# LoRA B of the first phase read by fours of experts over all 128 partitions, with small orders changed on four engines

## The chip, the cores and the metric

The kernel runs on one core of a Trainium2 chip. The metric is the device time of one execution in microseconds (us), as the median of three runs. A core has a matrix engine (TensorE, PE in the profile), three engines for elementwise work (VectorE or DVE, ScalarE or ACT, GpSimd or POOL), and a SyncE (SP) that here only issues transfers. All engines run their own program in order and meet through semaphores. Sixteen DMA engines move data between HBM, the on-chip buffer SBUF (128 partitions) and back.

## The reference, cut to what matters

Two layers act on x of 32 x 64 x 1024 floats. The first, which holds the change, is

```
y   = agg_w(cond) @ x + agg_b(cond)                 # a mixing matrix and a bias per batch entry
A_eff = einsum('bn,nri->bri', gate, lora_A)         # 16 experts, rank 32, 8 groups b
B_eff = einsum('bn,nor->bor', gate, lora_B)         # lora_B: 16 experts x 1024 outputs x 32 ranks
x   = x + y @ kernel + bias + B_eff (A_eff y) + lora_B_shared (lora_A_shared y)
```

The second layer is a grouped convolution of x with a bias from cond, a gated product (w12, silu) and an output product (w3), added to x. All is computed to float32 accuracy: each operand of a large product is split into a high and a low part, and three products of parts are added.

## The kernel before, in words

There are four stages: the first layer (to about 250 us), the convolution, the gated product and the output product. The change lies in the first 60 us, where the operands of the first layer are made.

**Weights.** The 1024 x 1024 kernel is loaded in eight blocks of 128 rows (`load_wk(k)`, 512 KB each) into four slots `raw`. ACT copies a block into its high part (`wk_hi_part`, L808), DVE subtracts to get the low part (`wk_lo_part`, L1062; POOL does block 0, L726) and then frees the slot. Slot 0 is used by block 0, then by the shared LoRA B (`RAW_LBS`), then by block 7; blocks 4, 5 and 6 take slots 1, 2 and 3 after blocks 1, 2 and 3.

**LoRA A.** `la_result(0..3)` on PE multiplies the gates with LoRA A; `la_hi_part` (ACT, L791) and `la_lo_part` (DVE, L1057) split the results.

**LoRA B.** Its output index is split into z, b and e (2 x 32 x 16 values). It is read in two halves z of 1 MB each, into `lb_raw[z]` of 128 partitions x 8 KB. Partition 32a + b holds, for the four experts 4a + n, the 16 outputs e of block b. Before, one DMA per a fills 32 partitions with four runs of 2 KB each. DVE turns each half with 8 transposes in two calls (`turn_lora_b`, L1153), calls 2 and 3 for half z = 1 and calls 0 and 1 for half z = 0. `lb_result_mm(0..3)` on PE multiplies with the gates: 0 and 1 need turns 2 and 3, and 2 and 3 need turns 0 and 1 as well. `lb_hi_part` (ACT, L820) and `lb_lo_part` (DVE, L1158) split the four results.

**Shared LoRA B.** 32 partitions x 4 KB; DVE turns it (L1173), ACT and POOL make its high and low part.

**PE.** After two tiles of y (`y_tile(0)`, `y_tile(1)`: y of 128 rows each, in banks 0 and 1), the first two row tiles go through their eight k steps `first_u(a, k)` one block of weights at a time, between the LoRA products. `first_u(0, 0)` writes bank 2 and so waits for `bias_made` 2, the convolution's bias `cb_c`, which DVE takes from that bank. `first_u(1, 0)` writes banks 4 and 5, and waits until DVE has made `la_lo_part(0)` and `(1)` from them. After k = 7 come `z_group(0)` and the steady loops.

**SP's order.** SP issues nearly every transfer of this phase, in one order, and waits in it for slots. After `wk_lo_part(6)` frees a slot (wait before `load_x(3, 3)`, L382) come the rest of y's bias (L430), the first group's LoRA B rows (`first_group_lb`, L358), b3, the eight stores of LoRA B to `lora_b_scratch` (L438), x tiles 4 and 5, then a wait for these stores and the loads of the next group's LoRA B (L455, L457), for which PE waits in `u_tile(2, ...)`. ACT issues the second half of the first group's rows.

Of the kernel before, what the change touches and what calls it, by code (L numbers as in the profile page):

```python
# [26 lines left out]
ALU = mybir.AluOpType  # L27
# [4 lines left out]
NB, NC, NL = 32, 64, 1024  # L32
# [7 lines left out]
NLORA, RANK = 16, 32  # L40
# [3 lines left out]
PH, BLK = 8, NL // 8  # L44
# [6 lines left out]
def layered_kernel(nc, x, cond, fside, c0_w0, c0_b0, c0_w1, c0_b1, c0_w2, c0_b2, c0_weight, c0_bias_k,  # L51
# [17 lines left out]
    with ctx:  # L69
        BASE = -(-nc.sbuf_base // 64) * 64  # L70

        def at(name, shape, kb, dt=F32):

            return nc.alloc_sbuf_tensor_at(name, shape, dt, offset=BASE + int(kb * 1024))

        def sem(name):
            return ctx.enter_context(nc.semaphore(name))
# [55 lines left out]
        def tiny(name, shape):  # L133
            k = next(small)
            for _ in range(-(-4 * int(np.prod(shape[1:])) // 32) - 1):
                next(small)
            return at(name, shape, k / 32)
# [4 lines left out]
        fside_s = tiny("fside_s", [NB, NC])  # L142
        yb_c, cb_c = tiny("yb_c", [NB, NC]), tiny("cb_c", [NB, NC])
# [60 lines left out]
        def bank(n, k=1):  # L204
            return ps[:, n * HALF:(n + k) * HALF]
# [24 lines left out]
        bias_mm, bias_made = sem("bias_mm"), sem("bias_made")  # L230
# [15 lines left out]
        lb_in = [sem(f"lb_in{c}") for c in range(2)]  # L246
# [45 lines left out]
        RAW_LBS, QUART = 4, HALF // 2  # L292
# [7 lines left out]
        def wait_slot(eng, n):  # L300

            if n in POOL_WK:
                eng.wait_ge(wk_lo_pool, n + 1)
            else:
                eng.wait_ge(raw_free, n + 1 - len(POOL_WK))


        lb_raw = [at(f"lb_raw{s}", [P, 2 * NL], k) for s, k in enumerate((144.25, 82))]
# [55 lines left out]
        def _(sp):  # L364
            def load_raw(n, src, rows=P):
                if n >= 4:
                    wait_slot(sp, n - 4)
                sp.dma_start(raw[n % 4][0:rows, :], src).then_inc(raw_in[n % 4], 16)
# [9 lines left out]
            def load_wk(k):  # L378
                load_raw(raw_of(k), f0_kernel[k * P:(k + 1) * P, :])
# [14 lines left out]
            def store_bias(n, src, stored):  # L394
                sp.wait_ge(bias_made, n + 1)
                sp.dma_start(bias_dram[n].rearrange("(b o) -> b o", o=NC), src[:, :]).then_inc(stored, 16)


            lb_v = lora_b.rearrange("(a n) (z b e) r -> z a b n (e r)", n=4, z=2, b=32)

            def load_lora_b(z):
                for a in range(4):
                    sp.dma_start(lb_raw[z][32 * a:32 * a + 32, :].rearrange("b (n e) -> b n e", n=4),
                                 lb_v[z, a]).then_inc(lb_in[z], 16)

            load_lora_b(1)
            load_raw(RAW_LBS, lora_b_s.rearrange("(b o) r -> b (o r)", b=32), rows=32)
            store_bias(0, yb_c, yb_stored)
            load_wk(4)
            load_lora_b(0)  # L410
            load_wk(5)
            store_bias(1, cb_c, cb_stored)
            load_wk(6)
# [362 lines left out]
        def _(act):  # L776
# [11 lines left out]
            def la_hi_part(n):  # L788

                act.wait_ge(lora_mm, n + 1)  # L790
                act.activation(la_hi[:, 2 * n:2 * n + 2, 0:NG * RANK],  # L791
                               bank(LA_BANKS[n]).rearrange("p (a c) -> p a c", a=2), ACT.Copy).then_inc(la_hi_made, 1)
# [11 lines left out]
            def wk_hi_part(k):  # L804

                n = raw_of(k)
                act.wait_ge(raw_in[n % 4], 16 * (n // 4 + 1))
                act.activation(wk_hi[:, k, :], raw[n % 4][:, :], ACT.Copy).then_inc(wk_hi_made, 1)  # L808
# [32 lines left out]
            wk_hi_part(2)  # L841
            la_hi_part(1)
            wk_hi_part(3)
            act.wait_ge(lbs_turned, 1)
            act.activation(lbs_c[0][:, :].bitcast(F32R), lbs_t[:, :], ACT.Copy).then_inc(lbs_made, 1)
            la_hi_part(2)
            wk_hi_part(4)
            la_hi_part(3)
            wk_hi_part(5)
# [184 lines left out]
        def _(dve):  # L1034
# [20 lines left out]
            def la_lo_part(n):  # L1055
                dve.wait_ge(la_hi_made, n + 1)
                dve.tensor_tensor(la_lo[:, 2 * n:2 * n + 2, 0:NG * RANK], bank(LA_BANKS[n]).rearrange("p (a c) -> p a c", a=2),  # L1057
                                  la_hi[:, 2 * n:2 * n + 2, 0:NG * RANK], ALU.subtract).then_inc(lora_taken, 1)

            def wk_lo_part(k):  # L1060
                dve.wait_ge(wk_hi_made, k + 1)
                dve.tensor_tensor(wk_lo[:, k, :], raw[raw_of(k) % 4][:, :], wk_hi[:, k, :], ALU.subtract).then_inc(wk_lo_made, 1)  # L1062
                dve.wait_ge(wk_lo_made, k + 1 - len(POOL_WK))
                dve.sem_inc(raw_free, 1)
# [43 lines left out]
            def add_bias(t, first=False):  # L1108

                for h in range(2):  # L1110
                    dve.wait_ge(y_mm, t * 2 + h + 1)
                    if not first:
                        dve.wait_ge(y_lo_made, t * 2 + h - 1)
                    dve.tensor_tensor(y_f[h][:, :].rearrange("p (k r) -> p k r", r=P),  # L1114
                                      bank(h).rearrange("p (k r) -> p k r", r=P),
                                      y_bias[:, ds(t * P, P)].unsqueeze(1).to_broadcast([P, 4, P]), ALU.add).then_inc(y_taken, 1)

            def y_rest(t, s, a):
                for h in range(2):
                    dve.wait_ge(y_hi_made, t * 2 + h + 1)  # L1120
                    dve.tensor_tensor(y_lo[s][:, a, 4 * h:4 * h + 4, :].rearrange("p k r -> p (k r)"),
                                      y_f[h][:, :], y_hi[s][:, a, 4 * h:4 * h + 4, :].rearrange("p k r -> p (k r)"),
                                      ALU.subtract).then_inc(y_lo_made, 1)
# [35 lines left out]

            dve.wait_ge(yb_made, 1)  # L1160
            add_bias(0, True)
            y_rest(0, 0, 0)
            add_bias(1)
            dve.wait_ge(bias_mm, 2)
            dve.tensor_tensor(cb_c[:, :], bank(2)[0:NB, NC:2 * NC], fside_s[:, :], ALU.add).then_inc(bias_made, 1)  # L1165
            y_rest(1, 0, 1)
            wk_lo_part(1)
            la_lo_part(0)
            wk_lo_part(2)
            la_lo_part(1)  # L1170
            wk_lo_part(3)
            dve.wait_ge(raw_in[RAW_LBS % 4], 16 * (RAW_LBS // 4 + 1))
            dve.transpose(lbs_t[:, :].rearrange("p (b o q) -> p o q b", b=32, q=PH),  # L1173
# [282 lines left out]
            for u in range(HALF_UNITS + 1, GATE_UNITS - 1):  # L1456
                n, k = u - 1, (u - 9 if u <= 12 else None)
# [126 lines left out]
        def _(pe):  # L1584
# [45 lines left out]
            def conv_bias():  # L1630
                pe.wait_ge(setup_chain, 7)
                pe.wait_ge(bias_made, 1)
                mm(bank(2)[0:NB, NC:2 * NC], emb_t[:, :], cw_t[:, :], True, True).then_inc(bias_mm, 1)
# [11 lines left out]
            def lb_result_mm(n):  # L1645

                m = LB_ORDER[n]
                pe.wait_ge(lb_turned, 2 * (n // 2) + 2)
                dst = bank(LB_BANKS[n])
                for odd in range(2):  # L1650
                    src = lb_t[:, 2 * (m % 2) + odd, 2 * (m // 2):2 * (m // 2) + 2].rearrange("p c q b -> p (c q b)")
                    last = mm(dst[64 * odd:64 * odd + 64, :], gate_e[:, :, :].rearrange("p g r -> p (g r)"), src,
                              True, True)
                last.then_inc(lora_mm, 1)


            def y_tile(t, slot, loaded, first=False):

                pe.wait_ge(x_loaded[slot], loaded)
                for h in range(2):  # L1660
                    if not first:
                        pe.wait_ge(y_taken, t * 2 + h - 1)
                    for k in range(4):
                        c0 = (4 * h + k) * P
                        last = mm(bank(h)[:, k * P:(k + 1) * P], x_in[slot][:, c0:c0 + P],
                                  mix[:, ds(t, 1), :].rearrange("p a r -> p (a r)"), True, True)
                    last.then_inc(y_mm, 1)
# [39 lines left out]
            def first_u(a, k):  # L1707

                pe.wait_ge(y_lo_made, 2 * a + 1 + k // 4)
                if k in POOL_WK:  # L1710
                    pe.wait_ge(wk_lo_pool, k + 1)
                else:
                    pe.wait_ge(wk_lo_made, k + 1 - len(POOL_WK))
                return u_step(k, 0, a)
# [23 lines left out]
            pe.wait_ge(mix_made, 8)  # L1738
            pe.wait_ge(yb_made, 1)
            y_tile(0, 0, 16, True)  # L1740
            y_tile(1, 1, 16)
            conv_bias()
            pe.wait_ge(bias_made, 2)
            first_u(0, 0)
            pe.wait_ge(gate_made, 1)
# [12 lines left out]
            dst, dst1 = first_u(0, 3), first_u(1, 3)  # L1758
            lb_result_mm(0)
            lb_result_mm(1)  # L1760
            pe.wait_ge(lora_taken, 4)
            lb_result_mm(2)
            lb_result_mm(3)
            for k in range(4, 8):
                dst, dst1 = first_u(0, k), first_u(1, k)
            pe.wait_ge(lora_taken, 4 + 3)
            z_group(0, 0, True)
# [186 lines left out]
```

## Time and profile before

| what | value |
| --- | --- |
| median of 3 runs | 800.48 us (798.65 to 801.49) |
| the profiled execution | 804.9 us, span 803.1 us |
| PE busy | 779.6 us, 97% of the span |
| DVE, ACT, POOL busy | 526.9, 208.9, 83.9 us |
| mean granted clock of PE | 0.989 |

The span is the time from the first to the last instruction; the execution's own time is 1.8 us longer. PE's busy time is a modelled one and includes overlapping ends, so a busy PE is not PE at its peak. `PEclk` 1.00 in the tables is TensorE's full clock of 2.4 GHz, 0.50 is 1.2 GHz. Times in the rows are from the start of the span. "Idle before, releaser" is what an engine waited for.

### The profile page before, as it was taken

To read this page: it belongs to the slowest core of one execution; us is meant where nothing else is said; L and a number is where in the kernel's file an instruction comes from. 1 tells how busy PE (TensorE), PEld (TensorE's weight loads), DVE (VectorE), ACT (ScalarE), POOL (GpSimd) and SP (SyncE) were. 2 spreads that over 40 slices of the span, in tenths; PEclk is the share of its full clock that TensorE was granted. 3 is DMA by queue.
4 is the path that set the end of the run, shared out by engine and by line. 5 is a ranking of instruction groups with operands and counts; after the bars stand their busy time and mean duration, and the time that the engine had idled before them with its cause. 6 is when DMAs were issued, how large, how long until landed. Compare 5 with 4: busy or idle time off the path is not lost.

```text
span 803.1 us, 10383 instructions
## 1 busy us (share of the span) xinstructions
PE 779.6 (97%) x3881; PEld 656.0 (82%) x3881; DVE 526.9 (66%) x636; ACT 208.9 (26%) x254; POOL 83.9 (10%) x56
## 2 busy tenths in 40 slices
PE   7988799999999999989999999999999999999998
PEld 5757688888888899868888888888888888888886
DVE  4656695436344379987777769877754796655552
ACT  5431010100000030433333337333333742111110
POOL 3141452231322100000000000000000000000000
PEclk9999999999999999989999999999999999999999
DMA  8967763464575799345444214278773664444441
GB/s 231 213 202 225 194 183 94 124 151 110 139 157 134 175 244 246 108 111 143 139 137 131 79 69 178 78 219 242 223 242 111 226 244 158 158 166 174 157 169 66
DMA packets 87275, 131.45 MB, mean 164 GB/s; under 512 B 11080, under 2 KB 64824, under 8 KB 84552
## 3 DMA queue, kind: packets, MB, share of 16 engines
q1 hardware_dynamic: 84064, 129.93, 56.1%
q10 hardware_dynamic: 3064, 0.90, 0.6%
q8 instruction: 20, 0.33, 0.2%
q0 software_dynamic: 112, 0.17, 0.1%
q14 instruction: 15, 0.12, 0.0%
HBM read 78.20 MB, written 51.72 MB: 162 GB/s over the span
## 4 chain that ended last, share of the span: by engine, by line
PE 81%; DMA 9%; DVE 6%; SPq 3%; issue 1%; ACT 1%; POOL 0%; DVEq 0%
PE ps L1827 37%; PE ps L1589 25%; PE ps L1887 19%; DMA raw<-in_L_ffn_lora_B_shared 2%; DMA raw<-in_L_ffn_kernel 2%; DVE cr L1293 2%; DMA lora_b_scratch<-lb_c_lo 1%; DMA a_scratch<-w_a_f 1%; DVE cf L1299 1%; DVE cf L1285 1%; SPq L358 1%; DMA lb<-lora_b_scratch 1%; SPq L438 1%; DMA c_scratch<-c_st 1%; DVE c_st L1299 1%
## 5 line engine op out<-in xcount | busy, mean ns | idle before, releaser
L1827 PE MATMUL ps<-cr,w_s_hi 128*128 128x512 f32 x512 | 159.8, 394 | 4.1 <-ACT s L919 4.1
L1827 PE MATMUL ps<-cr,w_a_hi 128*128 128x512 f32 x384 | 118.4, 389 | 0.0
L1827 PEld LDWEIGHTS ps<-cr,w_s_hi 128*128 128x128 f32 x512 | 97.3, 190 | 25.2 <-issue 4.9
L1827 PE MATMUL ps<-cr,w_s_lo 128*128 128x512 f32 x256 | 100.6, 393 | 0.0
L1827 PEld LDWEIGHTS ps<-cr,w_a_hi 128*128 128x128 f32 x384 | 72.0, 188 | 14.9
L1589 PE MATMUL ps<-wk_hi,y_hi 128*128 128x512 f32 x256 | 81.1, 398 | 2.0 <-DVE cb_c L1165 1.2
L1589 PE MATMUL ps<-wk_lo,y_hi 128*128 128x512 f32 x256 | 79.2, 391 | 0.0
L1589 PE MATMUL ps<-wk_hi,y_lo 128*128 128x512 f32 x256 | 78.8, 389 | 0.0
L743 POOL TENSOR_TENSOR x_t<-x_in,f_bias 128x1024 f32<-128x1024 f32 x16 | 63.5, 3973 | 137.5 <-DMA x_scratch<-x_t 137.5
L1146 DVE TENSOR_TENSOR x_t<-ps,x_t 128x1024 f32<-128x1024 f32 x16 | 19.5, 1223 | 86.7 <-PE ps L1589 86.7
L1827 PE MATMUL ps<-cr,w_a_lo 128*128 128x512 f32 x192 | 74.7, 389 | 0.0
L1518 DVE TENSOR_TENSOR res<-ps,res 128x512 f32<-128x512 f32 x56 | 38.5, 689 | 54.3 <-PE ps L1887 54.3
L815 ACT ACTIVATE y_hi<-y_f 128x512 fp32r<-128x512 f32 x32 | 19.5, 632 | 178.4 <-DVE y_f L1114 178.3
L1378 DVE TENSOR_TENSOR s<-ps,s 128x512 f32<-128x512 f32 x48 | 33.1, 689 | 41.6 <-PE ps L1827 41.3
L1589 PEld LDWEIGHTS ps<-wk_hi,y_hi 128*128 128x128 f32 x256 | 46.8, 189 | 13.0 <-issue 2.3
L1589 PEld LDWEIGHTS ps<-taps,x 128*128 128x128 f32 x512 | 57.3, 192 | 0.1
L1589 PE MATMUL ps<-taps,x 128*128 128x128 f32 x512 | 57.3, 275 | 0.0
L1827 PEld LDWEIGHTS ps<-cr,w_s_lo 128*128 128x128 f32 x256 | 48.6, 190 | 10.3
L1589 PEld LDWEIGHTS ps<-wk_lo,y_hi 128*128 128x128 f32 x256 | 48.3, 189 | 10.3
L1589 PEld LDWEIGHTS ps<-wk_hi,y_lo 128*128 128x128 f32 x256 | 48.1, 188 | 10.3
L919 ACT ACTIVATE s<-ps 128x512 f32<-128x512 f32 x48 | 28.6, 595 | 90.5 <-PE ps L1827 90.4
L925 ACT ACTIVATE s<-s,b_s 128x512 f32<-128x512 f32 x32 | 23.0, 719 | 79.7 <-DVE s L1378 79.7
(174 smaller groups left out, 1242.5 us busy)
## 6 DMA issues: line engine op xcount, KB each, us to landing
x_scratch<-x_t SPq DMA_DIRECT2D x128, 64.5 KB, 2.1
x<-x_scratch SPq DMA_DIRECT2D x32, 258.0 KB, 6.6
x_in<-in_x SPq DMA_DIRECT2D x16, 512.0 KB, 5.8
r_scratch<-r_t SPq DMA_DIRECT2D x16, 512.0 KB, 3.1
h_scratch<-s SPq DMA_DIRECT2D x32, 256.0 KB, 2.3
h_f<-h_scratch SPq DMA_DIRECT2D x8, 1024.0 KB, 5.9
res<-r_scratch SPq DMA_DIRECT2D x16, 512.0 KB, 5.0
raw<-in_L_ffn_w SPq DMA_DIRECT2D x56, 128.0 KB, 4.4
```

Of the source, the lines that this page charges most:

```text
L743: pool.tensor_tensor(blocks(x1_t[s]), x_in[slot][:, :].rearrange("p (b h q) -> p h q b", h=2, q=4), fb_v, ALU.add).then_inc(xb_made, 1)
L815: act.activation(y_hi[s][:, a, 4 * h:4 * h + 4, :].rearrange("p k r -> p (k r)"), y_f[h][:, :], ACT.Copy).then_inc(y_hi_made, 1)
L919: act.activation((s1[u % 2], s2[u % 2], s3)[n][:, :], bank((x, x, y)[n]), ACT.Copy).then_inc(part_copied, 1)
L925: act.activation(dst[:, :], dst[:, :], ACT.Silu, bias=b12_s[:, 0, j:j + 1]).then_inc(silu_made, 1)
L1146: dve.tensor_tensor(blocks(x1_t[s]), bank(2 + 2 * s, 2).rearrange("p (b h q) -> p h q b", h=2, q=4), blocks(x1_t[s]), ALU.add).then_inc(x1 ...
L1293: dve.tensor_tensor(cr[lo][:, :, :].rearrange("p b e -> p (b e)"), cf[f][:, :, :].rearrange("p b e -> p (b e)"), cr[hi][:, :, :].rearrange ...
L1299: return dve.tensor_tensor(dst.rearrange("p (q g o) -> p q g o", q=4, g=GRP), src, c_bias[:, b * NC:(b + 1) * NC].rearrange("p (g o) -> p ...
L1378: dve.tensor_tensor(dst[:, :], bank((w, x, y)[n]), dst[:, :], ALU.add).then_inc(part_added, 1)
L1518: dve.tensor_tensor(cols, bank(OUT_BANK[b] + s), cols, ALU.add).then_inc(out_made, 1)
L1589: return pe.matmul(o, l, r, start=start, stop=stop)
L1827: last = pe.matmul(o, l, r, start=first and q == 0 and n == 0, stop=q == 3 and n == 2, skip_group_check=True)
L1887: last = pe.matmul(o, l, r, start=first and k == 0 and n == 0, stop=k == QH - 1 and n == 2, skip_group_check=True)
```

## The change

It changes how LoRA B is read: one DMA per n (instead of per a) writes one run of 2 KB on each of the 128 partitions. The bytes, their places in SBUF and their number per DMA (256 KB) are the same. The shared LoRA B is issued ahead of both halves, and the half z = 0 ahead of block 4 instead of behind it. ACT does `la_hi_part(2)` ahead of the shared LoRA B's high part; DVE takes `cb_c` before `y_rest(0)` and does `la_lo_part(1)` ahead of `wk_lo_part(2)`; PE does `conv_bias` between the two y tiles, and both `first_u(., 4)` before `lb_result_mm(2)` and `(3)`.

```diff
-            lb_v = lora_b.rearrange("(a n) (z b e) r -> z a b n (e r)", n=4, z=2, b=32)
+            lb_v = lora_b.rearrange("(a n) (z b e) r -> z n a b (e r)", n=4, z=2, b=32)
             def load_lora_b(z):
-                for a in range(4):
-                    sp.dma_start(lb_raw[z][32 * a:32 * a + 32, :].rearrange("b (n e) -> b n e", n=4),
-                                 lb_v[z, a]).then_inc(lb_in[z], 16)
-
+                for n in range(4):
+                    cols = slice(n * 2 * PH * RANK, (n + 1) * 2 * PH * RANK)
+                    sp.dma_start(lb_raw[z][:, cols], lb_v[z, n]).then_inc(lb_in[z], 16)
+
+            load_raw(RAW_LBS, lora_b_s.rearrange("(b o) r -> b (o r)", b=32), rows=32)
             load_lora_b(1)
-            load_raw(RAW_LBS, lora_b_s.rearrange("(b o) r -> b (o r)", b=32), rows=32)
             store_bias(0, yb_c, yb_stored)
+            load_lora_b(0)
             load_wk(4)
-            load_lora_b(0)
             load_wk(5)
...
             wk_hi_part(3)
+            la_hi_part(2)
             act.wait_ge(lbs_turned, 1)
             act.activation(lbs_c[0][:, :].bitcast(F32R), lbs_t[:, :], ACT.Copy).then_inc(lbs_made, 1)
-            la_hi_part(2)
             wk_hi_part(4)
...
             add_bias(0, True)
+            dve.wait_ge(bias_mm, 2)
+            dve.tensor_tensor(cb_c[:, :], bank(2)[0:NB, NC:2 * NC], fside_s[:, :], ALU.add).then_inc(bias_made, 1)
             y_rest(0, 0, 0)
             add_bias(1)
-            dve.wait_ge(bias_mm, 2)
-            dve.tensor_tensor(cb_c[:, :], bank(2)[0:NB, NC:2 * NC], fside_s[:, :], ALU.add).then_inc(bias_made, 1)
             y_rest(1, 0, 1)
             wk_lo_part(1)
             la_lo_part(0)
+            la_lo_part(1)
             wk_lo_part(2)
-            la_lo_part(1)
             wk_lo_part(3)
...
             y_tile(0, 0, 16, True)
+            conv_bias()
             y_tile(1, 1, 16)
-            conv_bias()
...
             lb_result_mm(0)
             lb_result_mm(1)
+            dst, dst1 = first_u(0, 4), first_u(1, 4)
             pe.wait_ge(lora_taken, 4)
             lb_result_mm(2)
             lb_result_mm(3)
-            for k in range(4, 8):
+            for k in range(5, 8):
                 dst, dst1 = first_u(0, k), first_u(1, k)
```

## Rows read from the trace of the kernel before

**Rows 1.** The page, part 1: an engine's busy time, share, instructions.

```profile
PE 779.6 (97%) x3881; PEld 656.0 (82%) x3881; DVE 526.9 (66%) x636; ACT 208.9 (26%) x254; POOL 83.9 (10%) x56
```

**Rows 2.** The chain that ended last, first 120 us: start, length, what.

```profile
13.38 19.35 DMA raw<-in_L_ffn_lora_B_shared
...
34.90 11.71 DMA raw<-in_L_ffn_kernel
46.64 1.06 ACT wk_hi L808
...
48.68 4.01 DVE lb_c_lo L1158 x4
53.90 0.36 SPq L382
...
68.35 11.22 DMA lora_b_scratch<-lb_c_lo
...
88.54 31.67 PE ps L1589 x163
```

**Rows 3.** Stretches: busy us per engine, granted clock, DMA share, GB/s moved.

```profile
13.00:20.00 7.00, 6.61 (x46) 4.75 (x42) 4.70 (x9) 4.21 (x8) 0.35 (x1) 1.00 1.04 243
21.00:23.00 2.00, 1.86 (x10) 1.60 (x11) 1.41 (x4) 1.69 (x3) 0.00 (x0) 1.00 1.03 402
23.00:26.00 3.00, 3.00 (x29) 3.00 (x29) 1.88 (x2) 1.44 (x2) 0.00 (x0) 1.00 1.09 145
26.00:30.00 4.00, 3.50 (x17) 2.59 (x17) 3.05 (x3) 1.65 (x3) 0.00 (x0) 1.00 1.07 214
23.00:41.00 18.00, 17.50 (x108) 14.73 (x109) 11.58 (x17) 6.17 (x8) 2.93 (x2) 1.00 1.06 182
...
373.00:375.00 2.00, 2.00 (x10) 1.67 (x9) 2.00 (x3) 0.15 (x1) 0.00 (x0) 1.00 1.05 211
```

**Rows 4.** The timeline of PE: start, length, what, idle before and releaser.

```profile
19.65 0.30 PE L1589 MATMUL ps<-cw_t,emb_t 128*32 128x64 f32 x2
21.14 0.72 PE L1589 MATMUL ps<-wk_hi,y_hi 128*128 128x512 f32 x2 [1.19 <-DVE cb_c L1165]
...
28.26 0.73 PE L1589 MATMUL ps<-wk_hi,y_hi 128*128 128x512 f32 x2 [0.50 <-DVE la_lo L1057]
...
31.11 1.89 PE L1589 MATMUL ps<-gate_e,la_raw 128*128 128x64 f32 x16
...
40.31 1.94 PE L1589 MATMUL ps<-lb_t,gate_e 128*64 128x512 f32 x8
44.48 2.96 PE L1589 MATMUL ps<-lb_t,gate_e 128*64 128x512 f32 x8 [2.23 <-DVE lb_t L1153]
```

**Rows 5.** The timeline of DVE.

```profile
20.88 0.20 DVE L1165 TENSOR_TENSOR cb_c<-ps,fside_s 32x64 f32<-32x64 f32 x1
...
28.12 1.22 DVE L1062 TENSOR_TENSOR wk_lo<-raw,wk_hi 128x1024 fp32r<-128x1024 f32 x1
32.75 2.07 DVE L1173 STREAM_TRANSPOSE lbs_t<-raw 32x1024 f32<-32x1024 f32 x1 [3.42 <-DMA raw<-in_L_ffn_lora_B_shared]
...
41.60 2.73 DVE L1153 STREAM_TRANSPOSE lb_t<-lb_raw 128x256 f32<-128x256 f32 x8 [0.15 <-DVE wk_lo L1062]
```

**Rows 6.** The timeline of ACT.

```profile
37.59 0.60 ACT L791 ACTIVATE la_hi<-ps 128x512 fp32r<-128x512 f32 x1 [0.26 <-PE ps L1589]
...
47.60 3.72 ACT L820 ACTIVATE lb_c_hi<-ps 128x512 fp32r<-128x512 f32 x4
```

**Rows 7.** SP's queue: start of the issue, its length.

```profile
24.28 0.35 SPq L368 DMA_DIRECT2D raw<-in_L_ffn_kernel  x1
```

**Rows 8.** DMA issues between 24.2 and 24.5 us: count, KB, us to landing.

```profile
raw<-in_L_ffn_kernel SPq DMA_DIRECT2D x1, 512.0 KB, 11.6
```

**Rows 9.** Stretches around PE's idle time before 88.54 us, columns as in Rows 3.

```profile
84.50:88.50 4.00, 0.00 (x0) 0.00 (x0) 0.00 (x0) 0.00 (x0) 0.00 (x0) 1.00 1.00 225
89.80:93.10 3.30, 3.30 (x14) 2.91 (x13) 2.33 (x3) 1.26 (x2) 1.79 (x1) 0.51 0.81 181
```

## The prediction

> **What bounds the kernel now.** I read the page first. PE is busy for 97% of the span [rows 1], so over the whole kernel only what PE waits for, or what delays the steps on which it later waits, can give time. I then followed the chain that ended last through the first 120 us, since all edits lie ahead of 60 us. The reader is to see there that PE does not lead it before 88.54 us [rows 2]. It runs through the landing of the shared LoRA B (issued at 13.38, landed at 32.73), DVE's transpose, block 7 of the weights (issued at 34.90 when its slot came free, landed at 46.61), ACT's copy, the LoRA B splits on ACT and DVE, and `wk_lo_part(6)`, which lets SP go on at 53.90. From there SP's issues up to 68.35, the landing of the stores and the next group's loads follow without a gap until PE resumes at 88.54. All of that comes after the slot that `wk_lo_part(6)` frees, so I take it to move rigidly with it, and PE's own idle time ahead of 88.54 (4.0 us with no matmul [rows 9]) says that PE is not what ends there. The question is thus when `wk_lo_part(6)` is done; before, that is just ahead of 53.90.
>
> The second view, of stretches, says what made the landings late. From 21 to 23 us, with whole blocks of 128 partitions x 4 KB, the DMA moved 402 GB/s. When LoRA B began it fell to 145, then 214 GB/s, with a busy share of 1.05 to 1.09 [rows 3]. So the DMA engines were full but slow. From 23 to 41 us they moved 182 GB/s x 18 us = 3.28 MB, which is just the two halves (2.10), the shared part (0.13) and blocks 4 and 5 (1.05).
>
> **The change part by part.** *The small orders.* Before, PE's conv bias matmul ends at 19.95 and PE waits 1.19 us for `cb_c`, done at 21.08 [rows 4, 5]. With the matmul ahead of `y_tile(1)` and `cb_c` ahead of `y_rest(0)`, DVE takes it while PE is in `y_tile(1)`; `cb_c` delays `y_rest(0)` by its 0.20 us only, and that result is ready before PE ends the tiles. So `first_u(0, 0)` starts at 20.0, 1.1 us earlier. `la_lo_part(1)` no longer stands behind `wk_lo_part(2)` (1.22), which takes away the wait of 0.50 at 28.26 [rows 4, 5]; what is late instead is block 2's low part, by 0.7, and PE needs it 3 us after that.
>
> *PE's chain after.* From 21.14 to the end of `lb_result_mm(1)` at 40.31 + 1.94 = 42.25 PE has 21.11 us, less the wait of 0.50: 20.6 us of work [rows 4]. From 20.0 it ends at 40.6. Then come `first_u(0, 4)` and `(1, 4)`, a pair of steps, 31.11 - 28.26 = 2.85 [rows 4], and `lb_result_mm(2)`, `(3)`. These took 2.96 before, behind an idle time of 2.23; I take 1.94, as their twins at 40.31. PE is then at 40.6 + 2.85 + 1.94 = 45.4. ACT's split of result 3 is 3.72 / 4 = 0.93, DVE's 4.01 / 4 = 1.00, `wk_lo_part(6)` 1.22 [rows 2, 5, 6]: 48.6 instead of 53.9. **Gain 5.3 us**, if the data are there in time.
>
> *The data.* `first_u(0, 4)` at 40.6 needs in turn `wk_lo_part(4)` (1.22), `la_lo_part(3)` and `la_hi_part(3)` (0.6 each, the latter from the row, the former taken like it) and `wk_hi_part(4)` (1.06), since ACT and DVE do them in that order [rows 2, 5, 6]. So block 4 must land by 37.0. It landed at 24.28 + 11.6 = 35.9 before [rows 7, 8], and the change puts the half z = 0 ahead of it. Its arrival: from 23.0, the shared part 0.13 MB at the slow 145 GB/s, 0.9; two halves of 1.05 MB; block 4, 0.52 MB at 402, 1.3; and 0.5 for stragglers, my allowance. What one run of 2 KB on each of 128 partitions brings, no row shows. Bounds: the best is 402 GB/s, 2.6 us a half. The worst within what the layout says is no change; the 18 us less 0.9 and 2.6 for blocks 4 and 5 leave 14.5 us for both halves, 145 GB/s, slow tails included. Nearest is LoRA A, 13 to 20 us, also experts side by side on all 128 partitions with experts 128 KB apart in HBM: 243 GB/s [rows 3]. I take that, 4.3 a half: 23.0 + 0.9 + 8.6 + 1.3 + 0.5 = 34.3, so 2.7 us to spare. The gain is whole as long as both halves take no more than 37.0 - 23.9 - 1.8 = 11.3 us, 186 GB/s. Faster data add nothing, since PE's chain then sets the end.
>
> The row of 402 against those of 145 and 214 fits a rule of the Trainium skill, SBUF — State Buffer, section Door 1: The DMA port swizzle: a transfer to partitions 0 to 31 reaches 8 of 16 ports, with a limit of about 218 GB/s, one to all 128 reaches 16, about 436. By it a half would take an estimated 2.4 us, and the forecast would be the same. It does raise my chance that the rate goes up. Against the change speaks DMA: Bandwidth & Descriptors, section Latency and other measured facts: row pitches of large powers of two slow a copy, 512 KiB to 207 GB/s; the four experts of a transfer now lie 512 KB apart. By that figure a half would take an estimated 5.1 us, still inside the 11.3 for both.
>
> *The rest.* The shared part lands at about 24.5 instead of 32.7, so its transpose (2.07) follows `wk_lo_part(3)`, which ended at 28.12 + 1.22, without the wait of 3.42 [rows 5]; block 7 is issued at about 31 instead of 34.9, and lands after blocks 5 and 6 and f_bias (1.3 each) at about 39.5, ahead of the 43.4 at which ACT must begin its copy to be free for result 2. Turns 0 and 1 (2.73) end 2.8 us after `wk_lo_part(4)`, so 43.4 at the latest, and `lb_result_mm(2)` starts at 43.5: little to spare only if block 4 comes at its limit. `la_hi_part(2)` ahead of the shared split on ACT delays POOL and SP's shared copies by 0.6, under the 3 us by which they come earlier. Six issues that SP brings forward hold up nothing: it would wait for block 4's slot until 24.28 anyway. Together: 5.3 us.
>
> The profiled execution took 804.9, its span plus 1.8; 804.9 - 5.3 = 799.6. It lies 4.4 above the median of the runs, 800.48, so the median forecast is **795.2**.
>
> **The rivals.**
> 1. *The rate stays as it was* (the source order, not the partitions, made it slow). For: nothing here isolates the two; a load of 1 KB runs onto 32 partitions moves 211 GB/s at 373 us, no worse than the second half here [rows 3]. Against: the drop begins with the 32-partition transfers. Then block 4 lands at 23.9 + 14.5 + 1.8 = 40.2, 3.2 late, and as ACT and DVE have `la_hi_part(3)`, `la_lo_part(3)` and both turns behind it, PE waits as long. Gain 2.1: 798.4. Rates in between give 2 to 5.
> 2. *The gain is given back downstream.* For: the stores issued at 68.35 take 11.22 to land and the DMA moves 225 GB/s while PE idles [rows 2, 9]; if that backlog does not start earlier, PE resumes at the old time. Against: each transfer in it is issued behind the freed slot. Gain 0 to 2: about 800.
> 3. *Slower: four experts 512 KB apart are read much worse.* The price is twice the excess of a half. Past 11.3 + 5.3 = 16.6 us for both, 126 GB/s, the gain is gone; at half of LoRA A's 243, 17.3 us, the time is 0.7 longer; at 100 GB/s, 21 us, it is 4.4 longer, 804.9. For: LoRA A's 243 on 128 partitions shows that experts side by side do cost. Against: no stretch of the phase is under 145.
> 4. *The clock.* After PE's idle time at 84.5 it ran 3.3 us at a granted 0.51, half of 2.4 GHz, 1.65 us of work lost [rows 9]. That idle time stays; whether the drop falls alike may move any case by 1.7 either way.
>
> **How the numbers follow.** Whole gain 0.62 (795.2, own range 793.3 to 797); rate unchanged or little better 0.18 (796.5 to 799.5); given back 0.12; slower mechanism 0.08. The range 793.0 to 800.0 takes in the first two and half of the third. About 0.3%, 2.4 us, is what a measurement of this kernel can tell from no change. Faster: 0.62, two thirds of the second: 0.73. Within: 0.20. Slower: 0.07.
>
> **What would show it.** In the profile after: over 186 GB/s from 24 us to the end of LoRA B; PE's waits before `first_u(0, 0)`, `first_u(1, 0)` and `lb_result_mm(2)` gone or below 0.3; `lb_result_mm(3)` done near 45.4 with no drop of the clock before; SP going on near 48.6; PE resuming near 83.2. The prediction is wrong if PE waits ahead of `first_u(0, 4)` (block 4 late), or if SP is early and PE resumes at 88 all the same.

## The result, and the profile after

The changed kernel is slower: 815.91 us in the median of 6 runs (813.06 to 817.21) against 802.39 for the kernel before in the same comparison (6 runs, 798.65 to 806.88), a ratio of 1.0159 with a 95% interval of 1.0118 to 1.0199. The forecast was 795.2, with a range up to 800.0. One execution of the kernel with only the small orders (below) took 869.03 us at a mean granted clock of 0.852; its ratio leaves that execution out.

The stretches of the changed kernel, with the columns of [rows 3]:

```profile
20.00:22.00 2.00, 2.00 (x14) 1.74 (x13) 1.84 (x4) 1.55 (x4) 0.00 (x0) 1.00 1.04 414
26.00:36.00 10.00, 10.00 (x61) 8.60 (x60) 6.32 (x9) 1.99 (x3) 2.36 (x1) 1.00 0.27 102
39.00:46.00 7.00, 1.29 (x7) 0.14 (x2) 0.00 (x0) 0.00 (x0) 0.00 (x0) 0.96 1.04 245
...
46.00:59.50 13.50, 5.26 (x14) 3.89 (x16) 6.93 (x13) 6.48 (x7) 3.66 (x8) 0.52 0.54 146
...
48.00:52.00 4.00, 0.00 (x0) 0.00 (x0) 0.00 (x0) 1.31 (x2) 0.00 (x0) 0.50 0.26 105
```

The last two columns are the answer in short. While LoRA B is read, 26 to 36 us, the DMA's busy share is 0.27 and its rate 102 GB/s. Before, the share was over 1 and the rate 145 to 214 [rows 3]. 0.27 of sixteen engines is 4.3: by the share, which the profile gives for all engines together, four engines work and twelve have nothing to do. Per engine in use the rate is even good: 102 / 4.3 = 24 GB/s, against 414 / 16.6 = 25 in whole blocks (20 to 22 us). From 48 to 52 us, while PE waits for block 4, share and rate are again those of four engines.

SP's queue in the changed kernel:

```profile
13.39 10.02 SPq L404 DMA_DIRECT2D lb_raw<-in_L_ffn_lora_B  x4
23.45 2.57 SPq L396 DMA_DIRECT2D bias_scratch<-yb_c  x1
26.06 8.04 SPq L404 DMA_DIRECT2D lb_raw<-in_L_ffn_lora_B  x4
34.15 3.00 SPq L368 DMA_DIRECT2D raw<-in_L_ffn_kernel  x2
...
64.87 1.11 SPq L382 DMA_DIRECT2D x_in<-in_x  x2
```

Its issues themselves take long: 10.02 and 8.04 us for four, where four such issues take 2.5 to 4.9 us when sixteen engines share the work (the kernel of the first experiment). So block 4 is not even issued before 34.15, where it was issued at 24.28 [rows 7], and it lands 16.5 us later. ACT, DVE and PE of the changed kernel show who waits for it, one row of each timeline:

```profile
50.69 1.06 ACT L808 ACTIVATE wk_hi<-raw 128x1024 fp32r<-128x1024 f32 x1 [18.07 <-DMA raw<-in_L_ffn_kernel]
```

```profile
52.27 0.69 DVE L1057 TENSOR_TENSOR la_lo<-ps,la_hi 128x512 fp32r<-128x512 f32 x1 [14.61 <-ACT la_hi L791]
```

```profile
17.68 0.30 PE L1589 MATMUL ps<-cw_t,emb_t 128*32 128x64 f32 x2
17.91 2.05 PE L1589 MATMUL ps<-mix,x_in 128*128 128x128 f32 x16
19.72 0.71 PE L1589 MATMUL ps<-wk_hi,y_hi 128*128 128x512 f32 x2
...
38.35 1.94 PE L1589 MATMUL ps<-lb_t,gate_e 128*64 128x512 f32 x8
54.23 1.19 PE L1589 MATMUL ps<-wk_hi,y_hi 128*128 128x512 f32 x2 [13.95 <-DVE wk_lo L1062]
...
97.98 3.78 PE L1589 MATMUL ps<-mix,x_in 128*128 128x128 f32 x16 [3.82 <-DMA lb<-lora_b_scratch]
```

Up to 40 us PE goes as forecast: `first_u(0, 0)` starts at 19.72, without the wait that stands in [rows 4], and `lb_result_mm(1)` ends at 40.3, forecast 40.6. Then `first_u(0, 4)` waits 13.95 us. DVE names ACT's `la_hi` as the releaser, but that copy was not late by its own data (PE had made them by 35.6); it stood behind `wk_hi_part(4)`, which waited 18.07 us for block 4. PE's clock falls as well: in the stretch 46.0 to 59.5 us the granted clock was 0.52, after the idle time had begun at 40.3. `first_u(0, 4)` and `(1, 4)` then take 59.41 - 54.23 = 5.18 us, where a pair of steps took 2.85 before [rows 4]. SP goes on at 64.87 and PE resumes at 97.98, against 53.90 and 88.54 [rows 2].

### The profile page after: what moved, and what is told of

Read it like the earlier page. It is cut to its first block, busy times and chain, and to the rows that moved or that the text cites. A ratio compares the mean times of both kernels' runs of the same rounds, so it can differ in the third digit from the quotient of the medians.

```text
span 813.9 us, 10383 instructions
## 1 busy us (share of the span) xinstructions
PE 780.5 (96%) x3881; PEld 656.3 (81%) x3881; DVE 526.5 (65%) x636; ACT 208.7 (26%) x254; POOL 83.6 (10%) x56
## 4 chain that ended last, share of the span: by engine, by line
PE 82%; DVE 6%; DMA 6%; SPq 5%; issue 1%; ACT 1%; POOL 0%; DVEq 0%
PE ps L1828 36%; PE ps L1589 28%; PE ps L1888 18%; DMA raw<-in_L_ffn_kernel 3%; SPq L404 2%; DVE cr L1293 2%; DMA lora_b_scratch<-lb_c_lo 1%; DVE cf L1285 1%; DVE cf L1299 1%; DMA h_f<-h_scratch 1%; DMA lb<-lora_b_scratch 1%; SPq L358 1%; DVE c_st L1299 1%; SPq L438 1%; DVE w_a_f L1243 1%
## 5 line engine op out<-in xcount | busy, mean ns | idle before, releaser
L1589 PE MATMUL ps<-wk_hi,y_lo 128*128 128x512 f32 x256 | 79.5, 392 | 0.0
L1589 PEld LDWEIGHTS ps<-wk_hi,y_hi 128*128 128x128 f32 x256 | 47.0, 190 | 25.5 <-issue 16.6
L1589 PEld LDWEIGHTS ps<-wk_hi,y_lo 128*128 128x128 f32 x256 | 48.6, 190 | 10.5
L1589 PEld LDWEIGHTS ps<-wk_lo,y_hi 128*128 128x128 f32 x256 | 48.6, 190 | 10.5
```

Of the source, the lines that this page charges most:

```text
L1589: return pe.matmul(o, l, r, start=start, stop=stop)
```

## The experiments

The theories were: E, a transfer runs on as many DMA engines as the outermost dimension of its source allows, four in the change; P, the 512 KB between the experts of one transfer make the reads slow; O, the order, with block 4 behind both halves, is the loss at any rate.

**The source walked b first.** Still 2 KB on each of 128 partitions and experts 512 KB apart; only the outermost dimension is 32 instead of 4. The rows of LoRA B land on other partitions, and nothing after it is changed to fit, so this kernel does the same work but does not compute the reference's result. That holds for every version below with b first, and for the two next ones, with outermost dimension 8 and with experts 128 KB apart.

```diff
-            lb_v = lora_b.rearrange("(a n) (z b e) r -> z n a b (e r)", n=4, z=2, b=32)
+            lb_v = lora_b.rearrange("(a n) (z b e) r -> z n b a (e r)", n=4, z=2, b=32)
```

> The changed kernel with the source of each LoRA B transfer walked b first (32), then a (4), instead of a first: still one run of 2 KB on each of 128 partitions, still experts 512 KB apart. Rows land on other partitions, so LoRA B's rows are permuted in the result; the work is the same. Theory E (a transfer runs on as many DMA engines as the outermost dimension of its source allows: 4 in the change): the DMA share during LoRA B goes from 0.27 to about 1, its rate from 102 to 243 GB/s or more, block 4 lands near 34, PE's wait of 13.95 us goes, and the time is 795 to 798 (14 to 19 below the changed kernel). Theory P (the pitch of 512 KB makes the reads slow): rate and time stay, 813 to 817. Theory O (the order, block 4 behind both halves, is the loss whatever the rate): 808 or more.

Measured: 799.13 us (11 runs), ratio to before 0.9983 (0.9969 to 0.9998), some 17 us below the changed kernel, and 1.1 above the 795 to 798 expected. Its first trace was of a late execution (807.05 us: block 0 landed 2 us late, PE ran from 24 to 28 us at a granted clock of 0.50, SP went on at 55.08), with a share of 1.04 and 328 GB/s from 24 to 28 us; so it was profiled again.

> The kernel with the source walked b first (LoRA B's rows permuted in the result), once more, since block 0 landed 2 us late in its first trace and PE ran from 23 to 33 us at a granted 0.50. Theory E: without that, LoRA B moves at 243 to 400 GB/s and block 4 lands by 34; by the prediction's chain SP goes on at 48 to 49 and PE resumes near 82 to 83, as with the old transfers. Rival: the DMA finishes early but PE's and DVE's chain gives nothing back, and SP goes on at 50 or later.

In that execution, 798.2 us, a stretch of LoRA B reads:

```profile
24.00:28.00 4.00, 4.00 (x20) 3.11 (x20) 3.07 (x4) 2.01 (x3) 0.00 (x0) 1.00 1.05 382
```

```profile
48.45 1.11 SPq L382 DMA_DIRECT2D x_in<-in_x  x2
```

```profile
81.71 3.13 PE L1589 MATMUL ps<-mix,x_in 128*128 128x128 f32 x16 [2.53 <-DMA lb<-lora_b_scratch]
```

The share is back over 1, at 382 GB/s. PE does not wait for `first_u(0, 4)`, SP goes on at 48.45 and PE resumes at 81.71. P falls, since the pitch is the same, and O, since the order is; E gave the share and the rate.

**Outermost dimension 8.** Each transfer takes 8 experts x 16 blocks, 128 KB between experts.

```diff
-            lb_v = lora_b.rearrange("(a n) (z b e) r -> z n a b (e r)", n=4, z=2, b=32)
+            lb_v = lora_b.rearrange("(m a) (z y b e) r -> z m y a b (e r)", m=2, z=2, y=2, b=16)
...
-                    sp.dma_start(lb_raw[z][:, cols], lb_v[z, n]).then_inc(lb_in[z], 16)
+                    sp.dma_start(lb_raw[z][:, cols], lb_v[z, n // 2, n % 2]).then_inc(lb_in[z], 16)
```

> The changed kernel with each LoRA B transfer walked as 8 experts x 16 blocks of 2 KB (128 partitions; experts 128 KB apart; LoRA B's rows are permuted in the result). Theory E: an outermost dimension of 8 gives 8 engines: DMA share about 0.5 and about 200 GB/s while LoRA B moves alone, both halves in 10 to 11 us, block 4 lands at about 36 to 38 and the time is 798 to 803. Theory P (pitch): with 128 KB between experts, a share of 1 and 240 GB/s as LoRA A. A theory by which any first dimension below 16 falls to 4 engines or fewer: share 0.27, 813 to 817.

**Outermost dimension 4, experts 128 KB apart.**

```diff
-            lb_v = lora_b.rearrange("(a n) (z b e) r -> z n a b (e r)", n=4, z=2, b=32)
+            lb_v = lora_b.rearrange("(n a) (z b e) r -> z n a b (e r)", n=4, z=2, b=32)
```

> The changed kernel with neighbouring experts in one transfer: outermost dimension 4 as in the change, but 128 KB apart instead of 512 KB (LoRA B's rows are permuted in the result). Theory E: nothing changes, share 0.27 and 102 GB/s, 813 to 817. Theory P: the rate rises to that of LoRA A's loads, 240 GB/s, and the time falls below 803.

The same stretch of the first (outermost 8), and then of the second:

```profile
24.00:28.00 4.00, 4.00 (x24) 3.18 (x24) 2.94 (x5) 2.62 (x4) 0.00 (x0) 1.00 0.52 182
```

```profile
24.00:28.00 4.00, 4.00 (x23) 3.21 (x23) 2.94 (x5) 2.54 (x4) 0.00 (x0) 1.00 0.27 97
```

Share 0.52 is 8.3 engines, 0.27 is 4.3. With 4, 8 and 32 outermost the share is 0.27, 0.52 and 1.05: it follows that dimension until all sixteen engines are busy, and not the pitch. The medians were 806.68 us for 8 (10 runs, ratio 1.0063, 1.0029 to 1.0096) and 815.40 for 4 (4 runs, 1.0152, 1.0089 to 1.0214). The number for 8 engines missed my expectation of 798 to 803. ACT and a stretch of that kernel:

```profile
42.30 1.06 ACT L808 ACTIVATE wk_hi<-raw 128x1024 fp32r<-128x1024 f32 x1 [9.25 <-DMA raw<-in_L_ffn_kernel]
```

```profile
40.00:44.00 4.00, 0.72 (x4) 0.00 (x0) 0.12 (x1) 1.70 (x3) 0.00 (x0) 0.86 0.51 198
```

Block 4 landed at 42.3 and not by 38, though it was issued at 26.42. I had not counted that it shares the engines with the half ahead of it and with blocks 5 to 7. Around its landing the share is 0.51, that of eight engines, as it was that of four in the changed kernel: in both the last bytes move on as few engines as LoRA B has. That these are LoRA B's own engines, with parts of the blocks behind LoRA B on them, fits, but the profile does not name the engines.

**The parts by themselves.** First all the new orders, with LoRA B's transfers as before (the view and the loop over a of the kernel before put back into the changed one). Then the kernel before with only the new form of the transfers, four outermost; with only the form, but b first; and with only the small orders of DVE, ACT and PE (the edits of the diff ahead, taken alone).

> The changed kernel with all its orders, but LoRA B read as before (one transfer per a, 32 partitions, four runs each). Theory E: sixteen engines again, 145 to 215 GB/s; block 4 lands near 40 by the working of the prediction's first rival, PE waits about 3 us for its low part, gain 2 us against the kernel before: 798 to 802. Theory P: the same as E here, since experts are 128 KB apart. Theory O: block 4 late by as much as in the changed kernel, 808 or more.

> The kernel before with only the new form of the LoRA B transfers (one per n over 128 partitions); order of issue and all other orders as before. Theories E and P: DMA share 0.27 during LoRA B, block 4 is issued ahead of the half z = 0 but behind the half z = 1 on four engines, so it lands some 5 to 10 us late, and blocks 5 to 7 behind the second half: 808 to 818, slower than before by 1 to 2%. Theory O: within 0.5% of before, since the order is the old one.

> The kernel before with only the form of the transfers new, walked b first so that sixteen engines take part (LoRA B's rows permuted in the result). It is what the changed kernel's form would give if it did not fall to four engines. In the second trace of before DVE has no wait from wk_lo_part(4) on and SP goes on at 49.5, so faster data should save only what DVE waits for ahead of that: 0 to 1 us, 799.5 to 801. If landings are the bound in a typical execution too, 2 us or more.

> The kernel before with only the small orders of DVE, ACT and PE (LoRA B's transfers and SP's order as before). Theories E and P: PE starts first_u(0, 0) 1.1 us earlier, first_u(1, 0) does not wait, and the idle time of 2.2 us before lb_result_mm(2) is filled; but wk_lo_part(6) hangs on block 7, which lands at 46.6 as before, so the time is within 0.3% of before, at most 2 us less. Theory O says nothing of it. If it is slower by 0.3% or more, one of the small orders costs by itself.

| kernel | median us | ratio to before, 95% interval |
| --- | --- | --- |
| all new orders, old transfers | 800.18 | 0.9993 (0.9970 to 1.0016) |
| new form only, outermost 4 | 811.77 | 1.0151 (1.0092 to 1.0210) |
| new form only, b first | 799.14 | 0.9977 (0.9959 to 0.9996) |
| small orders only | 801.53 | 1.0003 (0.9979 to 1.0026) |
| all new orders, b first | 799.13 | 0.9983 (0.9969 to 0.9998) |

The form alone, with its four engines, brings the loss, under the old order as under the new (4 runs of the new form only). There PE waits for LoRA B itself, and not for block 4:

```profile
45.26 3.68 PE L1589 MATMUL ps<-lb_t,gate_e 128*64 128x512 f32 x8 [4.22 <-DVE lb_t L1153]
56.64 3.68 PE L1589 MATMUL ps<-lb_t,gate_e 128*64 128x512 f32 x8 [7.70 <-DVE lb_t L1153]
```

SP goes on at 64.72 there, at 64.87 in the changed kernel. The orders alone bring nothing that these runs can tell. With sixteen engines the form brings 0.2%, with or without the orders, in intervals that end just under 1; the 799.14 of the form alone lies a little below the 799.5 to 801 expected. The old transfers with the new orders lie in their expected range, but PE's wait of about 3 us was not there. So the expected gain of 5.3 us was not there even where the mechanism worked. Why, the next run shows.

**The kernel before once more.**

> The kernel before once more, for a second trace. Its first profiled execution took 804.9 us, 4 above the median of its runs, and landings in the first phase differ between executions of one kernel by 2 us and more. If the prediction's base (wk_lo_part(6) done at 53.9, PE resuming at 88.5) was that of a late execution, this trace shows it 2 to 5 us earlier, near 50 and 85, with a span of 799 or less; that would explain why the gain of 5 to 6 us in the trace of the kernel with the old transfers and all new orders is 0.6 us in the medians. If the base is typical, it shows 53 to 54 and 88 again.

Measured: 798.4 us in one execution, span 796.6. Rows of this second trace of the kernel before: a stretch, then DVE, then SP's queue, then PE.

```profile
24.00:26.00 2.00, 2.00 (x20) 2.00 (x20) 0.69 (x1) 1.35 (x2) 0.00 (x0) 1.00 1.10 229
```

```profile
42.96 1.18 DVE L1062 TENSOR_TENSOR wk_lo<-raw,wk_hi 128x1024 fp32r<-128x1024 f32 x1
44.30 4.01 DVE L1158 TENSOR_TENSOR lb_c_lo<-ps,lb_c_hi 128x512 fp32r<-128x512 f32 x4 [0.15 <-DVE wk_lo L1062]
48.15 2.64 DVE L1062 TENSOR_TENSOR wk_lo<-raw,wk_hi 128x1024 fp32r<-128x1024 f32 x2
```

```profile
49.51 1.10 SPq L382 DMA_DIRECT2D x_in<-in_x  x2
```

```profile
43.18 1.94 PE L1589 MATMUL ps<-lb_t,gate_e 128*64 128x512 f32 x8 [0.83 <-DVE lb_t L1153]
...
83.47 3.44 PE L1589 MATMUL ps<-mix,x_in 128*128 128x128 f32 x16 [2.77 <-DMA lb<-lora_b_scratch]
```

The same kernel, the same transfers, but 229 GB/s where the first trace had 134 in the same stretch:

```profile
24.00:26.00 2.00, 2.00 (x20) 2.00 (x20) 0.88 (x2) 1.44 (x2) 0.00 (x0) 1.00 1.05 134
```

The landings come earlier, the idle time before `lb_result_mm(2)` is 0.83 instead of 2.23 [rows 4], DVE, which had waited 3.24 us before `lb_c_lo` in the first trace, waits 0.15, and SP goes on at 49.51, not 53.90. The first trace, 804.9 us, was of a late execution. This rests on more than one trace: the kernel of the last experiment below is the kernel before up to this point, and there SP goes on at 50.04.

```profile
50.04 1.13 SPq L389 DMA_DIRECT2D x_in<-in_x  x2
```

**The stores of LoRA B on two queues.** Since PE had waited 2.5 to 4.6 us in every trace with sixteen engines for the next group's LoRA B, one more change was tried on top of the kernel with all new orders and the old transfers, and on the kernel before: ACT issues the stores of pair 1, and b3's load goes behind SP's stores.

```diff
+        def store_lb(eng, pair):
+            eng.wait_ge(lora_taken, N_LORA)
+            for hl in range(2):
+                for odd in range(2):
+                    eng.dma_start(lb_w[hl, odd, pair], lb_c[hl][pair][64 * odd:64 * odd + 64, :]).then_inc(lb_stored[pair], 16)
...
+            store_lb(sp, 0)
             wait_slot(sp, raw_of(7))
             sp.dma_start(b3_s[:, :], b3.partition_broadcast(P)).then_inc(b3_in, 16)
-            sp.wait_ge(lora_taken, N_LORA)
-            for pair in range(2):
-                for hl in range(2):
-                    for odd in range(2):
-                        sp.dma_start(lb_w[hl, odd, pair], lb_c[hl][pair][64 * odd:64 * odd + 64, :]).then_inc(lb_stored[pair], 16)
...
             first_group_lb(act, 1)
+            store_lb(act, 1)
```

> The kernel with the old transfers and all new orders, and besides: ACT issues the four stores of pair 1 of LoRA B behind its part of the first group's rows, and b3's load (512 KB) goes behind SP's four stores instead of ahead. In the trace of the kernel without this, SP goes on at 48.4, its last store is issued near 62.3, the stores land at 73.4 and PE waits 3.9 us for the next group's LoRA B until 81.6. If SP's issues and b3's bytes set that end, the stores land 2 to 4 us earlier, PE resumes near 78 to 79.5 and the time falls by 2 to 3: 797 to 798.5. If the DMA's backlog sets it (x tiles, y's bias, stores at 200 GB/s), less than 1 us. If PE is not ready by then, its wait goes from 3.9 to about 1 and the rest is lost.

> The kernel before with only that move of the stores and of b3's load. If SP's issues set when PE resumes, the gain is that of the kernel above, 2 to 3 us, since PE's wait was 2.8 us in the second trace of before; what it has more than this one is the worth of the small orders in the medians, expected 0 to 1 us.

With the new orders: 798.29 us, ratio 0.9954 (0.9932 to 0.9976), the one version here that computes the reference's result and has an interval below 1; it is 2% under the changed kernel. The time is in the range expected. On the kernel before: 800.28, 0.9990 (0.9967 to 1.0013), nothing, where 2 to 3 us were expected. PE of the first of the two:

```profile
62.27 2.64 PE L1593 MATMUL ps<-mix,x_in 128*128 128x128 f32 x16 [2.92 <-DVE y_f L1118]
66.73 3.75 PE L1593 MATMUL ps<-lb,z 128*128 128x512 f32 x8 [1.83 <-DMA lb<-lb_c_lo]
```

The wait at the next group's LoRA B is gone (its loads are issued at 72.70 instead of 73.39), but PE reaches that point only at 83.20, not near 78 to 79.5 as expected, and later than the 81.59 of the kernel without the move. Block 4 had landed at 37.15 instead of 35.37, SP went on at 49.86 instead of 48.43, and two waits ahead of that point, for y's bias and for the first group's rows, are 2.92 and 1.83 us instead of 1.62 and 0.68. The span, 796.4, is no shorter than without the move, 796.6. On the kernel before, PE's wait stays, 2.58 us, and it resumes at 83.40, against 83.47. So the traces show no gain. Why the medians differ all the same, and why the move needs the new orders for it, these runs don't settle.

## Why the prediction was wrong

**The step that failed is the lower bound of the rate.** The text said "the worst within what the layout says is no change", 145 GB/s. It priced bytes per partition and pitch, and took for granted that sixteen engines share each transfer. Measured: 102 GB/s at a share of 0.27, below both the bound and the 126 GB/s at which the third rival had put the turn to slower. Put into that rival's own working, both halves at 102 take 20.6 us, 9.3 over the allowed 11.3; block 4 lands at 46.3, and the forecast would have been 4.0 us slower than before. The rival had the place and the sign, but the wrong cause: at 128 KB between experts nothing changed. In the Trainium skill, DMA: Bandwidth & Descriptors, section Why a DMA increments its semaphore by 16 and not by 1, states the rule: the engines are the largest number up to 16 that divides the slowest dimension of both sides. The shares of 0.27, 0.52 and 1.05 for 4, 8 and 32 agree. The prediction cited another section of that page and missed this one, though the diff shows the dimension: `z n a b (e r)` with a = 4.

**What made it 13.5 us and not 4.** Three terms. Block 4 landed at 50.7 instead of 46.3, and PE waited 13.95 us instead of 9.3. The clock was no term of that rival, and the two steps after the wait took 5.18 us instead of 2.85, 2.3 more. These two close the sum: 13.95 + 2.3 = 16.3, and SP goes on at 64.87, 16.4 later than the 48.43 of the kernel with the old transfers and the same orders. The third term is the gain of 5.3 that the working sets against the loss and that was mostly not there (below). Against the second trace of before, PE resumes 98.0 - 83.5 = 14.5 us later; the medians differ by 13.5. The kernel before had 802.39 in that comparison and 800.4 to 800.8 in the later ones.

Why block 4 landed 4.4 us later than the rate gives is in part open. "Six issues that SP brings forward hold up nothing" failed as a statement on the queue: the eight took 10.02 and 8.04 us, and block 4 was issued 9.9 us later than before. But with outermost dimension 8 it was issued only 2.1 us later than before and still landed at 42.3, 5.1 after what 182 GB/s gives by the same working (37.2). So the held issue alone does not explain it. What both kernels show is blocks 4 to 7 sharing the engines with what is left of LoRA B; the sum gave block 4 all sixteen engines at 402 GB/s. No run separates the two.

**PE's chain was right.** With sixteen engines SP goes on at 48.43 (old transfers) and 48.45 (b first), forecast 48.6; `first_u(0, 0)` starts without a wait; PE resumes at 81.59 and 81.71, forecast 83.2. "Faster data add nothing" held as well: 228 and 382 GB/s from 24 to 28 us give the same 48.4. Rows of the kernel with the old transfers:

```profile
48.43 1.13 SPq L382 DMA_DIRECT2D x_in<-in_x  x2
```

```profile
81.59 3.07 PE L1589 MATMUL ps<-mix,x_in 128*128 128x128 f32 x16 [3.87 <-DMA lb<-lora_b_scratch]
```

Not every execution reaches that: the kernel with the stores moved, the same up to this point, goes on at 49.86, after block 4 came at 37.15.

**The gain of 5.3 was mis-sized** because its base, 53.9, belonged to one late execution. Up to SP's going on, three traces are of the kernel before: 53.90, 49.51 and 50.04. Two are of the new orders with the old transfers: 48.43 and 49.86. Without the late one the new orders are between 0.4 us later and 1.6 us earlier, and the medians show 0.6 us (0.9993), inside their interval. The two traces of the kernel before differ by 6.5 us (804.9 and 798.4), and 53.90 - 49.51 = 4.4 of these lie ahead of SP's going on, in part in the waits that the sum took away: the 2.23 before `lb_result_mm(2)` was 0.83, while the 1.19 and 0.50 were there again. The prediction noted that the profiled execution lay 4.4 us above the median and subtracted the whole gain from the median all the same; it should have asked whether the waits it priced were what made that execution late.

The first rival (rate unchanged, block 4 at 40.2, PE waits 3.2) did not come about in the kernel with the old transfers and the new orders: ACT starts block 4 at 35.37 and PE does not wait. Its 145 GB/s came from the late execution too; these transfers moved 228 GB/s from 24 to 28 us. The second (given back downstream) was not seen: from SP's going on to PE's resuming it takes 33.1 to 35.2 us in every trace in which PE waits there, against 34.6 in the first trace of before.

## What to carry to other kernels

Read a new transfer's outermost dimension before its bytes: a DMA whose source starts with a dimension of 4 used four engines of sixteen here, and no other merit of its shape made up for that. A version of the change that uses sixteen engines and also puts LoRA B's rows where the kernel needs them was not run. A DMA share of about 0.25 or 0.5 while something waits for data is the sign of it in a profile. And where the profiled execution lies above the median, take a second trace before pricing an idle time in it: the idle time may be what made it late.

## What the runs showed of the hardware

Issuing is held as well as moving: SP's single issues of LoRA B took 2.4 us in the median and up to 5.7 us with four engines in the changed kernel, and up to 10.8 in the one with only the new form, against 0.6 in the median and up to 1.7 with sixteen (b first); what stood behind them in the queue was issued late. The rate of one and the same set of transfers differed between executions, 134 and 229 GB/s from 24 to 26 us, for no cause that the traces show. When blocks 4 to 7 joined LoRA B, 39 to 46 us of the changed kernel, all engines were busy at only 245 GB/s, where whole blocks move at 402 to 414 (21 to 23 us before, 20 to 22 after); that too stays open.
